# Gathers of the first graph layer: a wait for landed rows at every second block, and more blocks allowed ahead

## The chip, the cores and the metric

The kernel runs on one core of a Trainium2 chip. The metric is the device time of one execution in microseconds (us). Five engines work side by side: TensorE (PE), VectorE (DVE), ScalarE (ACT), GpSimd (POOL) and SyncE (SP), each with its own instruction stream, tied together by semaphores.

## The reference

Two graph layers over 12,500 nodes with 64 features and 400,000 edges, sorted by target node. Cut to what matters for the change, the first layer is:

```python
h0 = relu(layernorm(x))
src_feats = h0[src]                                   # one row per edge
h = concat([src_feats, edge_attr_32]) @ W1 + b1       # 400000 x 64
h = silu(layernorm(h) * g1 + be1)
messages = silu(h @ W2 + b2)
agg = segment_sum(messages, dst, 12500)
x = x + layernorm(silu(concat([agg, h0]) @ Wu + bu))
```

The second layer gathers and sums rows again and applies a two-matrix network. The change does not touch it.

## The kernel before, in words

The kernel first multiplies the node rows with the node part of W1 and stores the product as a table in HBM (`ptab`, "layer0_rows"). Layer 0 then needs, per edge, the table row of its source node plus the product of its 32 edge features.

The edges are cut into 391 blocks of 1024 (128 partitions by 8 columns, `BC` = 8). Block n uses slot s = n % 4 (`UN` = 4) of its buffers. The code is unrolled: `rounds` (L836) calls `step(e, j)` for eight blocks at a time, and each engine's `step` handles the block that is `lag` blocks behind (`lagged`, L824). The order of the work on each engine is thus written out by hand, and semaphores that count blocks tie the engines.

What each engine does for block n:

- SP (L885 to L892) loads the edge features, 128 KB, into slot s of `ea`, once the edge sums that read the slot have been made (`g_ep`).
- GpSimd (L896 to L906) waits until `g_z` (blocks whose edge sums are ready) has reached n - AHEAD + 1, with AHEAD = 2 (L872): the sums of block n - 2 have been made. Then `gather` (L737 to L742) issues eight indirect DMAs, each of which fetches 128 rows of 256 bytes into one column of slot s of `gat`. Each adds 16 to `g_gat[s]` when it has landed. The indices come from ACT, four blocks at a time (L803), two rounds ahead.
- PE multiplies the edge features (`edge_products`, L748, four matmuls); eight blocks later it transposes the normalised rows (L755, four), ten blocks later it makes the second product (L762 and L765, nine), thirteen blocks later it sums the messages into a window of target nodes (L772, eight). All of that is in one fixed order in `step` (L919 to L939).
- DVE adds the edge product in PSUM and the gathered rows (`z_ready`, L1000 to L1010; this is what raises `g_z`), which needs `g_ep` and `g_gat[s]`; it also takes the sums of squares of four blocks (L990), normalises (L1031), makes one-hot columns (L779) and adds the window sums (L812, L816).
- ACT squares four blocks at once (L953), applies the two silu functions (L967, L974) and converts indices (L803).

So a block's edge sum on DVE at L1008 needs two things: the gathered rows and PE's product of L748. GpSimd in turn needs an edge sum before it may go on.

```python
                        wait(pool, g_z, n - AHEAD + 1)
                        wait_alone(pool, "gpsimd")
                        gather(pool, ptab, j // UN, s, g_gat[s])
```

`wait_alone` raises a semaphore of its own, so that the wait stands on an instruction of its own.

Of the kernel before, what the change touches and what calls it, by code (L numbers as in the profile page):

```python
# [16 lines left out]
def build_gnn(nc, x, src, dst, src_rows, dst_rows, dst_heads, head_cols, edge_quads, W1, b1, g1, be1, W2, b2, Wu, bu, gn, bn, M1, c1, M2, c2, out):  # L17
# [8 lines left out]
    BLOCKS, BC = src.shape[1], src.shape[2]  # L26
# [36 lines left out]
    with ctx:  # L63
# [27 lines left out]
        def sem(name):  # L91
            return ctx.enter_context(nc.semaphore(name))
# [151 lines left out]
        def wait(eng, semaphore, value):  # L244

            if not isinstance(value, int) or value > 0:
                eng.wait_ge(semaphore, value)  # L247
# [10 lines left out]
        def wait_alone(eng, name):  # L258


            if name not in turns:
                turns[name] = sem(f"turns_of_{name}")
            eng.sem_inc(turns[name], 1)
# [473 lines left out]
        def gather(pool, table, half, j, done):  # L737

            for c in range(BC):
                pool.indirect_dma_start(  # L740
                    out=gat[:, j, c, :], out_offset=None, in_=table[:, :],
                    in_offset=bass.IndirectOffsetOnAxis(ap=idx[:, half, j, c:c + 1], axis=0)).then_inc(done, 16)  # L742
# [81 lines left out]
        def lagged(e, j, lag):  # L824

            return (j - lag) % UN, e * DB + j - lag

        def rows_before(e, j):

            return 2 * e + j // UN  # L830

        def there(n):

            return not isinstance(n, int) or 0 <= n < BLOCKS

        def rounds(step, lag):  # L836

            whole = BLOCKS // DB
            for e in range(whole):
                for j in range(DB):  # L840
                    step(e, j)
            for j in range(BLOCKS - whole * DB + lag):
                step(whole, j)

        def flagged(eng):
            return eng.value_load(flag[0:1, 0:1], min_val=0, max_val=1)
# [4 lines left out]
        g_gat = [sem(f"rows_gathered{j}") for j in range(UN)]  # L851
# [17 lines left out]

        NORMED, TURN, HID, SECOND, MSG, HOT, WSUM, WADD = 6, 8, 9, 10, 11, 11, 13, 14  # L870
        EARLY = 1
        AHEAD = 2  # L872

        def whole_round(e, j, back):

# [6 lines left out]
        with nc.Block() as block:  # L882
# [11 lines left out]
            @block.gpsimd  # L894
            def _(pool):
                def step(e, j):  # L896
                    s, n = lagged(e, j, 0)
                    if there(n):
                        if s == 0:
                            wait(pool, g_idx, rows_before(e, j) + 1)  # L900

                        wait(pool, g_z, n - AHEAD + 1)
                        wait_alone(pool, "gpsimd")
                        gather(pool, ptab, j // UN, s, g_gat[s])
                with pool.If(flagged(pool) == 0):
                    rounds(step, 0)  # L906

# [75 lines left out]
            def _(v):  # L983
                def squares_summed(e, j):

                    _, q = whole_round(e, j, 1)
                    if in_rounds(q):
                        wait(v, g_sq, q + 1)
                        wait(v, g_n, q * UN)
                        v.tensor_reduce(st[:, 0, :], sq[:, :, :, :].rearrange("p j c f -> p (j c) f"), X,  # L990
                                        ALU.add).then_inc(g_red, 1)

                def chain(e, j, k):

                    _, q = whole_round(e, j, 1)
                    if in_rounds(q):
                        wait(v, g_ra if k else g_red, q * RSTD + k if k else q + 1)
                        rstd_step(v, k, st[:, 0, :], st[:, 1, :], st[:, 2, :]).then_inc(g_ra, 1)
# [837 lines left out]
```

## Time and profile before

| what | value |
|---|---|
| median of 3 runs | 6933.1 us (6923.75 to 6956.05) |
| the profiled execution | 6930.31 us |
| span of its instructions | 6928.6 us |
| mean granted TensorE clock | 0.691 of full speed |
| GpSimd busy | 4280.7 us, 62% of the span |
| PE busy | 4087.1 us, 59% |
| DVE busy | 2515.7 us, 36% |
| ACT busy | 1807.5 us, 26% |
| GpSimd gathers of L740, both layers | 3992, 4050.5 us |
| HBM traffic over the span | 31 GB/s on average |

A page of the profile lists busy times by engine, the span in 40 slices, DMA queues, the chain that ended last and the costliest groups of instructions. Busy time on GpSimd here is the time in which it issues indirect DMAs. Other views list the instructions of one engine in order of time, each with the idle time ahead of it and what ended that idle time ("<-"); "issue" is idle time in which the engine waited for nothing that the profile shows, "remote" is a wait that ended with a semaphore whose writer the profile does not name. "Busy in a stretch" views give each engine's busy time and, in brackets, its number of instructions in a window of time.

### The profile page before, as it was taken

How to read it: one execution, taken by the hardware profiler on the slowest of the kernel's cores; microseconds unless marked ns; L12 is line 12 of the kernel's file. 1: busy time of each engine (PE TensorE's matmuls, PEld its weight loads, DVE VectorE, ACT ScalarE, POOL GpSimd, SP SyncE). 2: the span in 40 equal slices, each digit the busy share in tenths (PEclk: the TensorE clock that was granted, in tenths of full speed). 3: DMA queues.
4: the chain of work that ended last, by engine and by line, in shares of the span. 5: the costliest groups of instructions: out<-in, count | busy, mean ns of one | idle time of the engine just before them, and what ended most of it. 6: DMA issues, size and time to landing. Idle time of an engine off the chain costs nothing. (4 is left out here: it accounts for less than half of the span.)

```text
span 6928.6 us, 75131 instructions
## 1 busy us (share of the span) xinstructions
PE 4087.1 (59%) x24926; PEld 3298.2 (48%) x24926; DVE 2515.7 (36%) x5227; ACT 1807.5 (26%) x2517; POOL 4280.7 (62%) x4190
## 2 busy tenths in 40 slices
PE   5344544544554544555455455456658888788789
PEld 4233333433443433333334333335547777777776
DVE  5222222222222222222222222223656666566551
ACT  1011111111111111111111111111246555555551
POOL 3766666666666666666666666664456655556551
PEclk9556656666665666666566666666579999999995
DMA  2111111111111111111111111111110000000001
GB/s 84 42 34 34 34 34 34 35 33 34 34 35 33 35 34 34 35 34 35 33 34 34 33 35 35 33 34 23 40 23 18 18 17 16 17 17 17 17 17 34
DMA packets 257339, 216.92 MB, mean 31 GB/s; under 512 B 139070, under 2 KB 189563, under 8 KB 256617
## 3 DMA queue, kind: packets, MB, share of 16 engines
q0 software_dynamic: 133248, 136.74, 9.1%
q1 hardware_dynamic: 123881, 77.59, 3.9%
q8 instruction: 106, 1.74, 0.1%
q14 instruction: 104, 0.85, 0.0%
HBM read 199.53 MB, written 14.40 MB: 31 GB/s over the span
## 5 line engine op out<-in xcount | busy, mean ns | idle before, releaser
L740 POOL DMA_INDIRECT gat<-layer_rows,idx x3992 | 4050.5, 1015 | 2172.5 <-issue 1207.8
L765 PE MATMUL ps<-w2d,edge_buffers 128*128 128x128 f32 x3128 | 718.5, 348 | 868.9 <-issue 853.6
L1008 DVE TENSOR_TENSOR edge_buffers<-ps,gat 128x512 f32<-128x512 f32 x391 | 270.5, 692 | 2454.5 <-remote 1428.9
L1568 ACT ACTIVATE node_buffers<-ps 125x800 bf16<-125x800 f32 x1152 | 947.0, 838 | 703.8 <-PE ps L1619 553.5
L765 PEld LDWEIGHTS ps<-w2d,edge_buffers 128*128 128x128 f32 x3128 | 561.7, 241 | 1071.1 <-issue 1070.6
L772 PE MATMUL ps<-one_hots,edge_buffers 128*128 128x80 f32 x3128 | 604.4, 326 | 563.8 <-issue 543.2
L772 PEld LDWEIGHTS ps<-one_hots,edge_buffers 128*128 128x128 f32 x3128 | 593.4, 252 | 645.2 <-issue 615.5
L748 PE MATMUL ps<-w1e,edge_buffers 128*128 128x256 f32 x1564 | 616.0, 509 | 395.8 <-issue 263.1
L967 ACT ACTIVATE edge_buffers<-ps,gcol 128x512 f32<-128x512 f32 x391 | 302.6, 774 | 2088.1 <-remote 1730.9
L1619 PE MATMUL ps<-node_buffers 128*128 128x200 bf16 x4608 | 644.3, 265 | 333.3 <-ACT node_buffers L1568 188.3
L1598 PE MATMUL ps<-edge_buffers,node_buffers 125*128 125x192 bf16 x7200 | 811.5, 256 | 1.7 <-issue 1.2
L1598 PEld LDWEIGHTS ps<-edge_buffers,node_buffers 125*128 125x128 bf16 x7200 | 704.7, 142 | 16.5 <-issue 14.8
L1675 DVE TENSOR_TENSOR node_buffers<-iol,node_buffers 128x1024 bf16<-128x1024 bf16 x576 | 399.3, 693 | 633.4 <-PE ps L1619 454.1
L748 PEld LDWEIGHTS ps<-w1e,edge_buffers 128*128 128x128 f32 x1564 | 366.1, 255 | 521.9 <-issue 484.1
L1619 PEld LDWEIGHTS ps<-node_buffers 128*128 128x128 bf16 x4608 | 412.6, 102 | 420.0 <-issue 256.4
L755 PE MATMUL ps<-ident,node_buffers 128*128 128x128 f32 x1564 | 354.9, 329 | 402.5 <-issue 396.3
L1677 DVE TENSOR_TENSOR node_buffers<-ioh,node_buffers 128x1600 bf16<-128x1600 bf16 x576 | 567.8, 986 | 0.0
L974 ACT ACTIVATE edge_buffers<-ps 128x512 f32<-128x512 f32 x391 | 233.0, 596 | 976.7 <-remote 795.6
L755 PEld LDWEIGHTS ps<-ident,node_buffers 128*128 128x128 f32 x1564 | 241.1, 182 | 446.0 <-issue 443.3
L812 DVE TENSOR_TENSOR cT<-cT,ps 64x40 f32 x499 | 92.9, 186 | 901.8 <-remote 615.8
L953 ACT ACTIVATE node_buffers<-edge_buffers 128x2048 f32<-128x2048 f32 x98 | 187.2, 1910 | 837.1 <-DVE edge_buffers L1008 717.2
L1031 DVE TENSOR_TENSOR node_buffers<-edge_buffers,st 128x512 f32<-128x512 f32 x391 | 267.7, 685 | 3.3
(186 smaller groups left out, 2952.4 us busy)
## 6 DMA issues: line engine op xcount, KB each, us to landing
gat<-layer_rows,idx POOLq DMA_INDIRECT x3992
edge_buffers<-in_edge_quads SPq DMA_DIRECT2D x391, 128.0 KB
node_buffers<-in_x SPq DMA_DIRECT2D x5, 625.0 KB
layer_rows<-node_buffers SPq DMA_DIRECT2D x25, 125.0 KB
residual_rows<-node_buffers SPq DMA_DIRECT2D x5, 625.0 KB
layer_rows<-node_buffers SPq DMA_DIRECT2D x5, 625.0 KB
node_buffers<-residual_rows POOLq DMA_DIRECT2D x25, 125.0 KB, 4.4
out<-node_buffers SPq DMA_DIRECT2D x25, 125.0 KB
```

The source lines that it names most:

```text
L740: pool.indirect_dma_start(out=gat[:, j, c, :], out_offset=None, in_=table[:, :], in_offset=bass.IndirectOffsetOnAxis(ap=idx[:, half, j, c: ...
L748: mm = pe.matmul(o[:, k * 4 * F:(k + 1) * 4 * F], ea[:, j, k, :], w1e[:, :], start=True, stop=True)
L755: mm = pe.transpose(o[:, k * 128:(k + 1) * 128], zn[:, j, 2 * k:2 * k + 2, :].rearrange("p c f -> p (c f)"), ident[:, :])
L765: mm = pe.matmul(o[:, k * 128:(k + 1) * 128], hT[:, j, k * 128:(k + 1) * 128], w2d[:, :], start=False, stop=(k == PAIRS - 1), skip_group_c ...
L772: mm = pe.matmul(to[:, 0:2 * WIN], rows_of[:, 2 * k:2 * k + 2, :].rearrange("p c f -> p (c f)"), oh[:, j, 2 * k:2 * k + 2, :].rearrange("p ...
L967: a.activation(hT[:, s, :], tp[(j - HID) % 2][:, 0:PAIRS * 128], ACT.Silu, bias=gcol[:, 1:2], scale=gcol[:, 0:1]).then_inc(g_h, 1)
L1008: v.tensor_tensor(zb[:, j // UN % 2, s, :, :], zp[j % 2][:, 0:BC * F].rearrange("p (c f) -> p c f", c=BC), gat[:, s, :, :], ALU.add).then_ ...
L1568: a.activation(cnt[0:TP, s, ch * 8 * T:(ch + 1) * 8 * T].rearrange("p (b k) -> p b k", b=2), built[ch % 2][0:TP, :, :], ACT.Copy).then_inc ...
L1598: mm = pe.matmul(wide, cnt[0:TP, s, t:t + (GW - 1) * T + 1:T], hparts[:, t, :, :].rearrange("p k f -> p (k f)"), start=(t == 0), stop=(t = ...
L1619: mm = pe.matmul(built[ch % 2][:, i // 2, (i % 2) * 2 * T:(i % 2 + 1) * 2 * T], ohl[:, ch // 2 % 2, k // 2, :, k % 2], ohk[:, ch // 2 % 2, ...
L1675: v.tensor_tensor(ohl[:, g % 2, :, :, :], iol[:, :, :].unsqueeze(1).broadcast_to([128, GP // 2, 128, 2]), spread(keyl, d, g, 128), ALU.is_ ...
L1677: v.tensor_tensor(ohk[:, g % 2, :, :, :], ioh[:, :, :].unsqueeze(1).broadcast_to([128, GP // 2, 2 * T, 2]), spread(keyh, d, g, 2 * T), ALU ...
```

## The change

AHEAD goes from 2 to 4: the gathers of block n now wait for the edge sums of block n - 4 (whose slot of `gat` they overwrite) in place of those of block n - 2. And after the gathers of every block with an odd slot (n = 1, 3, ..., 389, 195 blocks) GpSimd waits until that block's eight gathers have landed, before it goes on to the next block.

```diff
         NORMED, TURN, HID, SECOND, MSG, HOT, WSUM, WADD = 6, 8, 9, 10, 11, 11, 13, 14
         EARLY = 1
-        AHEAD = 2
+        AHEAD = 4
...
                         wait(pool, g_z, n - AHEAD + 1)
                         wait_alone(pool, "gpsimd")
                         gather(pool, ptab, j // UN, s, g_gat[s])
+                        if s % 2 and n + 1 < BLOCKS:
+
+                            wait(pool, g_gat[s], rows_before(e, j) * (16 * BC) + 16 * BC)
                 with pool.If(flagged(pool) == 0):
                     rounds(step, 0)
```

`rows_before(e, j)` is the number of earlier blocks in the same slot, so the value waited for is that of the block just issued.

## Rows read from the trace of the kernel before

**Rows 1.** The page: busy time by engine, and the costliest gather and matmul groups.

```profile
PE 4087.1 (59%) x24926; PEld 3298.2 (48%) x24926; DVE 2515.7 (36%) x5227; ACT 1807.5 (26%) x2517; POOL 4280.7 (62%) x4190
...
L740 POOL DMA_INDIRECT gat<-layer_rows,idx x3992 | 4050.5, 1015 | 2172.5 <-issue 1207.8
L765 PE MATMUL ps<-w2d,edge_buffers 128*128 128x128 f32 x3128 | 718.5, 348 | 868.9 <-issue 853.6
```

**Rows 2.** Busy in a stretch, by stage: start, layer 0, its tail, the rest.

```profile
core 0: us, PE busy (x) PEld busy (x) DVE busy (x) ACT busy (x) POOL busy (x), PEclk, DMA share, GB/s
211.00:342.00 131.00, 35.39 (x90) 22.23 (x90) 19.85 (x42) 7.67 (x8) 98.66 (x104) 0.55 0.16 41
342.00:1000.00 658.00, 322.92 (x1377) 248.78 (x1378) 173.79 (x456) 101.61 (x141) 430.73 (x440) 0.60 0.14 34
1000.00:4772.00 3772.00, 1875.21 (x8057) 1417.02 (x8055) 999.30 (x2650) 579.28 (x804) 2524.16 (x2585) 0.62 0.14 34
4772.00:4800.00 28.00, 24.05 (x98) 19.84 (x98) 17.31 (x50) 9.89 (x13) 0.00 (x0) 0.50 0.06 3
4800.00:6929.00 2129.00, 1697.06 (x14550) 1483.65 (x14550) 1174.49 (x1833) 1069.63 (x1488) 1140.23 (x991) 0.84 0.10 21
```

**Rows 3.** The line of the gathers, L740, 205 to 4775 us: idle time ahead of them.

```profile
L740 POOL DMA_INDIRECT gat<-layer_rows,idx x3128: 941/947/1449, 211.5 to 4771.0; - x196
its engine sat idle before it (us, times) until:
  issue: 956.8, 3029
  DVE edge_buffers L1008: 550.1, 98
  ACT idx L803: 6.5, 1
```

**Rows 4.** POOL in order of time: the stops after runs of 24, 32 and 40 gathers.

```profile
2047.74 0.95 POOL L740 DMA_INDIRECT gat<-layer_rows,idx  x1 [0.30 <-issue]
2053.69 1.04 POOL L740 DMA_INDIRECT gat<-layer_rows,idx  x1 [5.00 <-DVE edge_buffers L1008]
...
2113.18 0.95 POOL L740 DMA_INDIRECT gat<-layer_rows,idx  x1 [7.41 <-DVE edge_buffers L1008]
...
2160.00 0.94 POOL L740 DMA_INDIRECT gat<-layer_rows,idx  x1 [5.98 <-DVE edge_buffers L1008]
...
2169.43 0.94 POOL L740 DMA_INDIRECT gat<-layer_rows,idx  x1 [0.30 <-issue]
```

**Rows 5.** Busy in a stretch, L740 alone: gathers in the runs before those stops.

```profile
core 0: us, POOL busy (x), PEclk, DMA share, GB/s
2113.00:2155.00 42.00, 31.39 (x32) 0.62 0.15 35
...
2018.00:2049.00 31.00, 23.25 (x24) 0.67 0.16 38
2053.00:2106.00 53.00, 38.73 (x40) 0.60 0.15 37
```

**Rows 6.** PE's pace after a stop that ended at 2113 us (columns as in rows 2).

```profile
2113.00:2123.00 10.00, 10.00 (x57) 8.48 (x56) 7.06 (x21) 2.07 (x4) 7.69 (x8) 0.80 0.16 39
2123.00:2133.00 10.00, 4.90 (x23) 3.33 (x23) 1.99 (x5) 2.69 (x3) 7.56 (x9) 0.71 0.15 37
2133.00:2144.00 11.00, 3.54 (x12) 2.60 (x10) 1.69 (x3) 0.60 (x1) 8.56 (x9) 0.50 0.16 39
2144.00:2154.00 10.00, 1.80 (x5) 0.93 (x5) 0.00 (x0) 0.00 (x0) 7.56 (x9) 0.50 0.12 26
```

**Rows 7.** PE and DVE in order of time: a product, and edge sums.

```profile
2177.09 1.44 PE L748 MATMUL ps<-w1e,edge_buffers 128*128 128x256 f32 x3 [0.42 <-issue]
...
2158.53 0.69 DVE L1008 TENSOR_TENSOR edge_buffers<-ps,gat 128x512 f32<-128x512 f32 x1 [1.86 <-remote]
...
2171.88 0.69 DVE L1008 TENSOR_TENSOR edge_buffers<-ps,gat 128x512 f32<-128x512 f32 x1 [3.57 <-DMA gat<-layer_rows,idx]
...
2205.31 0.69 DVE L1008 TENSOR_TENSOR edge_buffers<-ps,gat 128x512 f32<-128x512 f32 x1 [9.49 <-remote]
```

**Rows 8.** POOL and DVE in order of time: the stop at 342 us, after 104 gathers.

```profile
340.60 0.95 POOL L740 DMA_INDIRECT gat<-layer_rows,idx  x1 [0.31 <-issue]
358.76 1.04 POOL L740 DMA_INDIRECT gat<-layer_rows,idx  x1 [17.21 <-DVE edge_buffers L1008]
```

**Rows 9.** POOL and PE in order of time: a short stop at 3266 us.

```profile
3267.96 1.03 POOL L740 DMA_INDIRECT gat<-layer_rows,idx  x1 [1.96 <-issue]
...
3263.68 0.29 PE L772 MATMUL ps<-one_hots,edge_buffers 128*128 128x80 f32 x1 [0.90 <-issue]
3265.09 0.49 PE L772 MATMUL ps<-one_hots,edge_buffers 128*128 128x80 f32 x1 [1.12 <-issue]
3267.88 0.29 PE L772 MATMUL ps<-one_hots,edge_buffers 128*128 128x80 f32 x1 [2.29 <-issue]
3269.29 0.48 PE L772 MATMUL ps<-one_hots,edge_buffers 128*128 128x80 f32 x1 [1.12 <-issue]
3269.98 0.47 PE L755 MATMUL ps<-ident,node_buffers 128*128 128x128 f32 x1 [0.20 <-issue]
3270.68 0.37 PE L755 MATMUL ps<-ident,node_buffers 128*128 128x128 f32 x1 [0.22 <-issue]
```

## The prediction

> **What bounds the kernel now.** I read the page first, then the stages, then the gather line, then GpSimd, PE and DVE in order of time. The page shows no engine above 62% [rows 1], so a mean says little. The stages do: from 211 to 4772 us GpSimd issues the 3128 gathers of layer 0, and the rest of the kernel, which the change leaves alone, follows [rows 2]. Layer 0 is thus 4561 us, or 11.66 us for each of 391 blocks.
>
> GpSimd sets that pace. The gather line shows 3128 gathers and 956.8 + 550.1 + 6.5 = 1513.4 us of idle time ahead of them [rows 3]. Within a run the gap is 0.30 or 0.31 us; 3128 × 0.305 = 954 us is therefore the plain cost of going from one gather to the next. The other **559 us are stops**, nearly all ended by DVE's edge sum of L1008, 98 times. The rest, 4561 - 559 = 4002 us, is issue: 1.28 us per gather, 10.2 us per block. Extra per block now: 559 / 391 = 1.43 us, in stops of 5 to 7.4 us, about one every four blocks [rows 4].
>
> Why does the edge sum come late? Not for the rows: the last gather of a block ends at 2170.37 (2169.43 + 0.94) [rows 4] and its edge sum begins at 2171.88, released by the DMA [rows 7]: 1.51 us. It is late through PE. In the ten us after a stop PE starts 57 matmuls, then 23, then 12 in eleven us, then 5, while GpSimd issues at the same rate throughout [rows 6]. A block needs 25 (four of L748, four of L755, nine of L762 and L765, eight of L772), so 2.4 per us. PE keeps well ahead for 20 us of a run (80 matmuls, 3.2 blocks' worth) and then falls to a fifth of what is needed. Its idle time is "issue": it waits for nothing shown. What it reports is late as well: a product of L748 whose last matmul ends at 2178.5 releases an edge sum at 2205.31, marked "remote" [rows 7], 4.5 us after GpSimd has stopped. I read this as a debt: gathers issued without pause load something that PE's stream also needs, and only a pause of GpSimd pays it off.
>
> The debt has a size. The stop is 5.00 us after 24 gathers, 5.98 after 32, 7.41 after 40 [rows 4, 5], and 17.21 after the 104 gathers [rows 2] of the start, when PE had little to do [rows 8]. From 24 to 32 that is 0.12 us per gather; from 24 to 104 it is 12.2 / 80 = 0.15. A block of eight gathers so owes 0.98 to 1.22 us of GpSimd's silence, whenever it is paid. Of today's 1.43 us per block the remainder, 0.2 to 0.45, is what each stop costs besides: the edge sum itself (0.69) and GpSimd's restart, 0.78 us from the end of the sum (2158.53 + 0.69) to 2160.00 [rows 4, 7].
>
> **The change, part by part.**
> *AHEAD = 4.* No instruction is added or removed; the wait of block n asks for the sums of n - 4. Their slot is the one to be overwritten, so nothing else has to be free. The 98 stops on L1008 lose their reason as long as PE is less than two more blocks late, some 20 us. What is late next is the sum of n - 4. Behind GpSimd's wait only its own gathers are queued; SP's edge loads and ACT's indices don't wait for it. This part alone takes no debt away: it would make runs longer and each stop longer too.
> *The wait for landed rows*, 195 of them. No row shows GpSimd waiting for a DMA, so I bound it. From the end of a block's last issue to its release of DVE is 1.51 us [rows 4, 7]; GpSimd's restart after DVE adds 0.78 us, and the gap of 0.30 is there anyway. Upper value: 1.51 + 0.75 - 0.31 = 1.95 us. Lower value, if the restart lies inside the wait: 1.51 - 0.31 = 1.2, and the shortest stop shown, 1.96 us, would give 1.65 [rows 9]. I take 1.95, as every restart behind a semaphore in these rows has the 0.78. Sum: 195 × 1.95 = **380 us**. Queued behind it on GpSimd is the next pair's first gather; nobody else waits for it, since DVE has two landed blocks at that moment.
> *What it pays.* 380 us over 391 blocks is 0.97 us per block, against a debt of 0.98 to 1.22. The pauses come every 16 gathers, 20.5 us, the stretch in which PE still starts 80 matmuls against the 50 that two blocks need [rows 6]. So PE should stay in the good part of its curve. That a short pause helps is seen at 3266 us: with a stop of 1.96 us PE's matmuls go from 1.4 us apart to 0.7 us apart [rows 9], though it is not yet at full pace.
> *What is left over.* The unpaid part, 0.01 to 0.25 us per block, is 4 to 98 us, and comes as rarer stops on n - 4, each with some 1.5 us of its own (sum and restart). I take 50 us in all.
> *Clock, DVE, ACT, second layer:* PE's work in layer 0 is the same; its granted clock there is 0.60 to 0.62 [rows 2] between the two levels, and PE is not the bound, so nothing is charged. The tail from 4772 to 4800 stays.
>
> Sum: - 559 + 380 + 50 = - 129 us. Against the profiled execution, 6930.31 us, that is **about 6800**; it lies 3 us under the median of the runs, 6933.1.
>
> **A rule that speaks against it.** The row shows GpSimd held 1.51 us and a restart when it waits straight behind its issue. The Trainium skill ("DMA: Bandwidth & Descriptors", section "Rules for kernel authors") says to issue a DMA early, do other work, and wait on its semaphore late, so that the fixed cost overlaps; the change waits at once. The same page puts the fixed cost at about 2.0 us ("Anatomy of one DMA"); 195 times that is an estimate of 390 us added, with nothing given back. Whether that comes true is rival B, priced from rows.
>
> **The rivals.**
> *B: the pauses pay nothing, the stops stay (slower).* If a pause shorter than some 3 to 4 us does not release PE, PE still slows after 20 us of a run, whatever GpSimd does between. Place: the stops on L1008. They stay at one per four blocks with their length, since PE's rate per four blocks (some 100 matmuls per cycle of 2160.00 - 2113.18 = 46.8 us [rows 4]) hasn't changed, and AHEAD only shifts them. One of the two pauses per four blocks falls together with the stop, the other is added: 98 × 1.95 = 191 us, 7121 us. It decides from the point where PE's matmuls after a pause don't come closer together than before it. For it: at 3266 us PE didn't return to full pace after 1.96 us [rows 9]. Against: it doubled its pace, and that was after a long run, not after 16 gathers.
> *C: the debt is only moved (no change).* Each pause shortens the next stop by its own length, and the stops stay as frequent as PE's stock of 80 to 100 matmuls per run makes them. Then GpSimd's silence is the same 559 us: 6930. For it: the steady growth of the stop with the number of gathers, which knows no free payment.
> *D: the pauses do it all (faster still).* The debt never shows, there is no stop, and the wait costs 1.2 to 1.65 us: 559 - 234 to 559 - 380 less, 6605 to 6751. For it: in the first 131 us of layer 0 edge sums came on time for 13 blocks, while PE had few matmuls (90) [rows 2]. Against: the debt of at least 0.98 per block had to be paid in the end, 17.21 us [rows 8].
> That the change does nothing (the wait already satisfied when reached) is excluded: the wait stands behind the block's own issue, 1.5 us before it lands.
>
> **How the numbers follow.** Forecast 0.48; B 0.22; C 0.18; D 0.12. A measurement of this kernel can tell about 0.5%, 35 us, from no change. The forecast's own range is 6751 (nothing left over) to 6850 (98 us left over and its stops). The range asked for leaves out most of B above some 80 us and the lower part of D: 6690 to 7010. Faster by over 0.5%: forecast, D and an edge of C, 0.62. Within 0.5%: most of C and what joins from the forecast, 0.16. Slower: 0.22.
>
> **What would show it.** Right: GpSimd idle ahead of L740 in layer 0 about 1380 us in place of 1513; some 195 idle times of about 2.2 us ahead of a gather, released by the DMA or by "issue"; far fewer than 98 waits on L1008; PE's slices of ten us within layer 0 never down to 5 matmuls; the gathers of layer 0 end near 4640. Wrong: still 80 or more stops on L1008 of 5 us (B or C; C if they have become shorter by 2 us), or idle times of 3 us and more at the new wait, which would mean that landing reports are late in such runs too. Everything behind layer 0 must keep its 2129 us.

## The result, and the profile after

| | kernel before | changed kernel |
|---|---|---|
| median of the runs taken with the result | 6928.43 us (4 runs) | 6839.0 us (4 runs, 6821.14 to 6840.21) |
| ratio, 95% interval | | 0.9865 [0.9822, 0.9908] |
| the profiled execution | 6930.31 us | 6821.14 us |
| first to last gather of layer 0 | 4560.4 us | 4489.4 us |

The change makes the kernel 1.35% faster, about 90 us, in the direction and inside the range that were forecast (6800 in 6690 to 7010), with a gain about two thirds of the 129 us of the sum.

The changed kernel, busy by stage, answers to [rows 2] (L1008 has become L1011 here, the later lines are three further down too):

```profile
core 0: us, PE busy (x) PEld busy (x) DVE busy (x) ACT busy (x) POOL busy (x), PEclk, DMA share, GB/s
211.00:342.00 131.00, 36.03 (x96) 22.94 (x97) 19.62 (x42) 8.27 (x9) 91.82 (x96) 0.54 0.16 39
1000.00:4701.00 3701.00, 2160.11 (x7973) 1645.87 (x7973) 1001.54 (x2640) 571.86 (x795) 2536.79 (x2578) 0.56 0.14 35
4701.00:4749.00 48.00, 43.47 (x289) 36.78 (x290) 28.05 (x86) 19.55 (x27) 1.32 (x2) 0.86 0.04 4
```

The line of the gathers in layer 0 of the changed kernel, against [rows 3]:

```profile
L740 POOL DMA_INDIRECT gat<-layer_rows,idx x3128: 938/944/1443, 211.1 to 4699.6; - x196
its engine sat idle before it (us, times) until:
  issue: 1100.1, 2999
  DVE edge_buffers L1011: 191.8, 71
  DMA gat<-layer_rows,idx: 125.1, 57
  ACT idx L803: 5.6, 1
```

Idle time is 1422.6 us in place of 1513.4. With the plain 954 us taken off, GpSimd's silence has gone from 559 to **469 us**. Counted over the 3128 gathers, only 13 gaps of over 2.6 us are left, 61.7 us together (before: 97, 569.6 us), none of them between 1870 and 4113 us. Eight of the 13 stand at a new wait; the other 187 pauses have a median of 2.22 us from the end of a gather to the next. So most of the 71 waits that the view puts down to L1011 are pauses too, like the second one below.

GpSimd and DVE in order of time in the changed kernel: two pauses, a small gap after the first gather of a pair, and edge sums.

```profile
2145.08 1.38 POOL L740 DMA_INDIRECT gat<-layer_rows,idx  x1 [2.23 <-issue]
...
2167.71 1.38 POOL L740 DMA_INDIRECT gat<-layer_rows,idx  x1 [2.26 <-DVE edge_buffers L1011]
2170.51 0.94 POOL L740 DMA_INDIRECT gat<-layer_rows,idx  x1 [1.42 <-issue]
...
2144.36 0.69 DVE L1011 TENSOR_TENSOR edge_buffers<-ps,gat 128x512 f32<-128x512 f32 x1 [6.07 <-DMA gat<-layer_rows,idx]
2156.69 0.69 DVE L1011 TENSOR_TENSOR edge_buffers<-ps,gat 128x512 f32<-128x512 f32 x1 [10.31 <-DMA gat<-layer_rows,idx]
2166.99 0.69 DVE L1011 TENSOR_TENSOR edge_buffers<-ps,gat 128x512 f32<-128x512 f32 x1 [8.28 <-DMA gat<-layer_rows,idx]
```

The pair takes 22.63 us, and in these rows the edge sums wait for their gathered rows, as they should, and no longer for TensorE. Its pace in ten-us slices, against [rows 6]:

```profile
2100.00:2110.00 10.00, 5.40 (x25) 4.45 (x25) 1.01 (x4) 4.86 (x7) 7.73 (x8) 0.67 0.15 37
2110.00:2120.00 10.00, 7.07 (x25) 5.67 (x25) 2.05 (x5) 0.60 (x1) 7.55 (x8) 0.50 0.16 36
2120.00:2130.00 10.00, 5.30 (x17) 3.72 (x17) 4.95 (x9) 1.37 (x2) 6.11 (x6) 0.50 0.10 23
2130.00:2140.00 10.00, 6.99 (x26) 5.49 (x25) 3.63 (x14) 0.00 (x0) 7.76 (x8) 0.50 0.17 39
```

Here PE has 17 to 26 in each, at half clock for most of the time, and that is enough. Counted from 340 us on over the whole of layer 0, the slow slices have become rare but are not gone: of 435 slices, 80 have 12 matmuls or fewer (before: 210) and 10 have 5 or fewer (before: 86).

Where the 109 us between the two profiled executions come from: 71 from first to last gather of layer 0; about 7 behind its last gather (TensorE's backlog is smaller: the last matmul of L772 starts 50 us after the last gather ended before, 44 after); 33 from the first to the last gather of layer 1 (1647.9 us before, 1615.0 after). The change leaves layer 1's code alone, and another profile of the changed kernel has 1661.8 there, so the last term is scatter and no gain. (Behind the gathers of layer 1 the changed kernel takes 2 us more, which closes the sum.)

### The profile page after: what moved, and what is told of

It is laid out like the page before. It is cut to its first block and busy times, and to the rows that moved or that the text cites. A ratio compares the mean times of both kernels' runs of the same rounds, so it can differ in the third digit from the quotient of the medians.

```text
span 6819.3 us, 75228 instructions
## 1 busy us (share of the span) xinstructions
PE 4384.2 (64%) x24926; PEld 3521.7 (52%) x24926; DVE 2520.6 (37%) x5227; ACT 1807.0 (26%) x2517; POOL 4292.5 (63%) x4190
## 5 line engine op out<-in xcount | busy, mean ns | idle before, releaser
L740 POOL DMA_INDIRECT gat<-layer_rows,idx x3992 | 4061.0, 1017 | 2057.2 <-issue 1349.3
L748 PE MATMUL ps<-w1e,edge_buffers 128*128 128x256 f32 x1564 | 736.4, 608 | 988.0 <-DVE edge_buffers L1011 770.5
L1011 DVE TENSOR_TENSOR edge_buffers<-ps,gat 128x512 f32<-128x512 f32 x391 | 270.5, 692 | 2831.4 <-DMA gat<-layer_rows,idx 1590.4
L748 PEld LDWEIGHTS ps<-w1e,edge_buffers 128*128 128x128 f32 x1564 | 424.7, 298 | 1154.1 <-issue 1095.4
L765 PE MATMUL ps<-w2d,edge_buffers 128*128 128x128 f32 x3128 | 759.3, 390 | 328.3 <-issue 321.6
L772 PE MATMUL ps<-one_hots,edge_buffers 128*128 128x80 f32 x3128 | 693.1, 380 | 390.3 <-issue 241.7
L772 PEld LDWEIGHTS ps<-one_hots,edge_buffers 128*128 128x128 f32 x3128 | 676.4, 298 | 516.4 <-issue 478.1
L765 PEld LDWEIGHTS ps<-w2d,edge_buffers 128*128 128x128 f32 x3128 | 618.4, 279 | 512.6 <-issue 512.1
L755 PE MATMUL ps<-ident,node_buffers 128*128 128x128 f32 x1564 | 387.5, 376 | 182.5 <-issue 178.4
L755 PEld LDWEIGHTS ps<-ident,node_buffers 128*128 128x128 f32 x1564 | 292.7, 217 | 215.7 <-issue 215.1
```

Source lines behind the costliest of these rows:

```text
L740: pool.indirect_dma_start(out=gat[:, j, c, :], out_offset=None, in_=table[:, :], in_offset=bass.IndirectOffsetOnAxis(ap=idx[:, half, j, c: ...
L748: mm = pe.matmul(o[:, k * 4 * F:(k + 1) * 4 * F], ea[:, j, k, :], w1e[:, :], start=True, stop=True)
L755: mm = pe.transpose(o[:, k * 128:(k + 1) * 128], zn[:, j, 2 * k:2 * k + 2, :].rearrange("p c f -> p (c f)"), ident[:, :])
L765: mm = pe.matmul(o[:, k * 128:(k + 1) * 128], hT[:, j, k * 128:(k + 1) * 128], w2d[:, :], start=False, stop=(k == PAIRS - 1), skip_group_c ...
L772: mm = pe.matmul(to[:, 0:2 * WIN], rows_of[:, 2 * k:2 * k + 2, :].rearrange("p c f -> p (c f)"), oh[:, j, 2 * k:2 * k + 2, :].rearrange("p ...
L1011: v.tensor_tensor(zb[:, j // UN % 2, s, :, :], zp[j % 2][:, 0:BC * F].rearrange("p (c f) -> p c f", c=BC), gat[:, s, :, :], ALU.add).then_ ...
```

## The experiments

The experiments were run on five chips, and each ran beside the kernel before on its own chip; only those pairs are compared.

**1. AHEAD = 4 alone** (against the kernel before).

```diff
-        AHEAD = 2
+        AHEAD = 4
```

> AHEAD = 4, no wait for landed rows. Debt theory (every gather issued without pause adds 0.12 to 0.15 us to a debt that only silence of GpSimd pays): the silence per block stays at 0.98 to 1.22 us plus the fixed part of each stop, so the gain is small: 0 to 60 us under the kernel before, 6870 to 6930; the stops are longer (7 to 9 us) and fewer. Rival, more blocks allowed ahead is what gained: the whole 90 us, about 6840. Rival C (PE has a fixed stock per stop): no change, stops as frequent as before.

Measured: 5996.86 us beside a kernel before of 5998.14, ratio 1.0022 [0.9944, 1.0100]. On this chip both kernels take some 930 us less than the kernel before took in the first measurement. The gathers of layer 0 in this run:

```profile
L740 POOL DMA_INDIRECT gat<-layer_rows,idx x3128: 940/944/1397, 211.9 to 4191.8; - x196
its engine sat idle before it (us, times) until:
  issue: 953.0, 3127
  ACT idx L803: 5.8, 1
```

There is no stop at all: 3127 plain gaps, 953 us, just the plain cost of the prediction. And the same four stretches of TensorE as in [rows 6]:

```profile
2113.00:2123.00 10.00, 7.99 (x28) 5.81 (x27) 3.54 (x14) 0.00 (x0) 7.87 (x8) 0.58 0.19 39
2123.00:2133.00 10.00, 5.52 (x25) 4.29 (x25) 1.99 (x5) 5.64 (x8) 7.56 (x9) 0.77 0.19 37
2133.00:2144.00 11.00, 5.65 (x25) 4.74 (x25) 2.17 (x6) 1.37 (x2) 8.26 (x10) 0.66 0.18 38
2144.00:2154.00 10.00, 6.53 (x22) 4.92 (x23) 4.96 (x10) 0.00 (x0) 7.56 (x9) 0.50 0.19 40
```

TensorE starts 22 to 28 matmuls in each of them, with gathers issued at the same rate. Over the whole of layer 0 no slice of ten us has 5 or fewer, and 14 of 384 have 12 or fewer. Neither the clock nor the DMA traffic makes the difference: the granted clock in these slices is 0.50 to 0.77, as on the other chip (0.50 to 0.80), and the traffic 37 to 40 GB/s (there 26 to 39). So the slowing beside uninterrupted gathers doesn't come from the kernel alone but from the chip it meets. Each chip was measured at one time only, so a lasting property of the chip and a passing state of it aren't told apart. I call this one the free chip, the others the bound chips. Which kind a run met can be read from its kernel before: 6000 or 6920 to 6950 us.

**2. The wait alone, the wait at every block, and the wait at every third block,** all on the free chip. The edits are against the changed kernel:

```diff
-        AHEAD = 4
+        AHEAD = 2
```

> The wait at every second block with AHEAD = 2. Debt theory: the pauses pay, PE is hardly late, so the edge sums of n - 2 are there in most of the layer: within 40 us of the changed kernel, 6800 to 6880. Rival, both halves are needed: the sums of n - 2 are late again and again, each costing a stop on top of the pauses: 6930 or more.

```diff
-                        if s % 2 and n + 1 < BLOCKS:
+                        if n + 1 < BLOCKS:
```

> AHEAD = 4, the wait at every block, 390 pauses of 1.92 us beyond the plain gap = 749 us against 464 us of stops in the changed kernel. Debt theory: no stops left at all, and the layer costs 749 - 464 = 285 us more than the changed kernel: about 7120. Rival (more silence also speeds something else, PE being the limit): less than 100 us more.

```diff
-                        if s % 2 and n + 1 < BLOCKS:
+                        if n % 3 == 2 and n + 1 < BLOCKS:
```

> AHEAD = 4, the wait at every third block: 130 pauses of 1.92 = 250 us, 0.64 us per block, less than the debt of 0.98. Debt theory: the steady stretch without stops is gone, stops return until the silence per block is 1.0 to 1.3 again, time 6830 to 6900. Rival (what counts is that a pause comes at all, not how much is paid): no stops, 214 us less than the stops of the changed kernel, about 6630.

| run, free chip | us | ratio to the kernel before | gathers of layer 0, first to last | more than without pauses, per pause |
|---|---|---|---|---|
| AHEAD = 4 alone | 5996.86 | 1.0022 [0.9944, 1.0100] | 3980.9 | |
| 130 pauses | 6275.48 | 1.0521 [1.0380, 1.0661] | 4257.5 | 2.13 us |
| 195 pauses, AHEAD = 2 | 6493.62 | 1.0886 [1.0740, 1.1031] | 4477.3 | 2.55 us |
| 390 pauses | 6861.18 | 1.1500 [1.1347, 1.1654] | 4845.6 | 2.22 us |

None of the expectations for a bound chip could be judged here, but the price could: where nothing has to be paid, a pause is a plain loss of 2.1 to 2.6 us, somewhat over the 1.95 of the prediction. The pause itself is 1.99 us beyond the plain gap; in the run with 195 of them the other 0.56 us per pause are longer gathers behind it (the first one takes 1.38 us in place of 0.94) and 32 small gaps of 1.41 us ahead of the gather after that. With 195 pauses layer 0 takes 4477 us on the free chip and 4489 in the changed kernel on a bound one: with them, the two kinds of chip are alike in layer 0.

**3. The changed kernel again,** unchanged, to see whether the gain was the chip's.

> The changed kernel as it is, beside the kernel before on one chip, since the first four runs stood beside a kernel before of 5998 us in which the gathers never stopped. If the slow pace of TensorE is a state of the chip on which it runs and this chip does not show it: the pauses cost 195 x 1.95 us and pay for nothing, ratio 1.06 to 1.09, some 6380 to 6500 against 6000. If this chip shows it: ratio 0.98 to 0.99 as in the first measurement. Rival: what differed was the kernel before alone, and the change gives 6839 anywhere.

Measured, on a bound chip: 6845.73 against 6941.77 us, ratio 0.9855 [0.9808, 0.9901]. The first result is repeated. The changed kernel itself was not run on the free chip; that the rival ("6839 anywhere") falls is argued from the wait alone, which takes 6494 us there.

**4. AHEAD = 4 alone and the wait alone, on a bound chip.**

> AHEAD = 4 without the wait, once more, for a chip on which the kernel before takes some 6930 us and TensorE slows beside the gathers. Debt theory: silence per block stays 1.0 to 1.3 us, stops longer (7 to 9 us) and fewer, ratio 0.991 to 1.000. Rival, AHEAD alone is the gain: ratio 0.986. Rival, a fixed stock of TensorE per stop: 1.00 with as many stops as before. Where the kernel before takes 6000 us again: ratio 1.00 and no stops.

> The wait at every second block with AHEAD = 2, once more, for a chip of the slow kind. Debt theory: the pauses pay and the edge sums of n - 2 are there in most of the layer, ratio 0.982 to 0.992. Rival, the room of two more blocks is needed as well: the late sums cost stops on top of the pauses, ratio 1.00 or above. On a chip of the fast kind: 1.08 to 1.09.

Measured on one chip, kernel before 6923.12: AHEAD alone 6917.11 (a difference of 6 us, where the runs of each kernel spread over more than 100 us), the wait alone 6855.08, ratio 0.9905 [0.9883, 0.9927]. The gathers of layer 0 with AHEAD alone:

```profile
L740 POOL DMA_INDIRECT gat<-layer_rows,idx x3128: 940/944/1464, 211.8 to 4765.6; - x196
its engine sat idle before it (us, times) until:
  issue: 1163.6, 3058
  DVE edge_buffers L1008: 376.2, 69
  ACT idx L803: 5.7, 1
```

and with the wait alone:

```profile
L740 POOL DMA_INDIRECT gat<-layer_rows,idx x3128: 938/944/1452, 215.9 to 4706.8; - x196
its engine sat idle before it (us, times) until:
  issue: 1065.6, 2989
  DVE edge_buffers L1011: 203.8, 81
  DMA gat<-layer_rows,idx: 129.1, 57
  ACT idx L803: 5.7, 1
```

AHEAD alone leaves 98 gaps of over 2.6 us with a median of 6.33 us and a silence of 1545.5 - 954 = 592 us, no less than before. The runs between stops stay at four blocks (55 of 97) with more fives and threes. The wait alone leaves 9 such gaps and a silence of 450 us. From first to last gather layer 0 takes 4492 us with the wait alone, 4489 and 4496 in two profiles of the changed kernel. **The wait is the change; AHEAD adds nothing that these runs can tell.** The rival "room is needed as well" falls too.

**5. Silence in small pieces, first attempt.** No wait for rows, AHEAD = 4, a one-element clear on GpSimd ahead of every second gather:

```diff
             for c in range(BC):
+                if spaced is not None and c % 2:
+                    pool.memset(spare[c // 2 * 32:c // 2 * 32 + 1, spaced:spaced + 1], 0.0)
```

> AHEAD = 4, no wait; instead GpSimd clears one element ahead of every second gather, four per block, so that the silence is spread in small pieces of 0.3 to 0.6 us. It adds 4 x 0.3 to 4 x 0.6 = 1.2 to 2.4 us per block. On a chip of the slow kind, debt theory (any silence pays, in whatever pieces): no stops of several us are left, the layer takes 3128 x 1.28 us plus the pieces, ratio 0.987 to 1.05. Rival (only an unbroken pause in which the last gather has landed releases TensorE): the stops stay, 559 us besides the pieces, ratio 1.07 to 1.13. On a chip of the fast kind it shows the price of the pieces alone.

Measured: 6940.71 against 6923.12 us, ratio 1.0030 [1.0012, 1.0048], and 96 gaps of over 2.6 us (median 6.38). It does not test the question: a clear takes 0.095 us and in most places hides in the plain gap of 0.30; the gaps with a clear come to 50 us more than as many plain ones, nearly all of it in 31 gaps of over 1 us. With no pieces paid, the stops stay.

**6. Pieces that cost time.** A copy of 200 bf16 elements per partition ahead of every fourth gather:

```diff
             for c in range(BC):
+                if spaced is not None and c % 4 == 3:
+                    wait(pool, s_spare, 2 * spaced + c // 4 + 1)
+                    pool.tensor_copy(spare[:, 200:400], spare[:, 0:200]).then_inc(s_spare, 1)
```

> AHEAD = 4, no wait for landed rows; GpSimd copies 200 bf16 elements per partition ahead of every fourth gather, two per block, since the one-element clears of the run with spaced gathers hid in the plain gap. Each copy should part two gathers by some 0.5 to 0.8 us more than the plain gap: 1.0 to 1.6 us per block in pieces in which the last gather has not landed. Debt theory on a chip of the slow kind: the pieces pay, fewer than 20 stops of over 2.6 us, layer 0 takes 4002 us plus 391 x 1.0 to 1.6. Rival (only an unbroken pause until the rows have landed releases TensorE): some 95 stops stay beside the pieces, 7300 or more.

GpSimd in order of time, a piece and a stop (the gathers' line is L746 here):

```profile
2111.48 0.94 POOL L746 DMA_INDIRECT gat<-layer_rows,idx  x1 [0.30 <-issue]
2112.43 0.35 POOL L745 COPY spare<-spare 128x200 bf16<-128x200 bf16 x1
2112.95 0.97 POOL L746 DMA_INDIRECT gat<-layer_rows,idx  x1 [0.17 <-issue]
2118.63 1.04 POOL L746 DMA_INDIRECT gat<-layer_rows,idx  x1 [4.70 <-DVE edge_buffers L1016]
```

A piece adds 0.22 us to the plain gap, a third of what I had expected: 782 of them, 188 us in all with the few longer ones. Measured: 6933.29 against 6953.33 us, ratio 0.9991 [0.9962, 1.0021]. The profiled execution is the shortest of the eleven (6839.91 us), but what it lacks lies behind the last gather of layer 1 (128 us, against 200 to 226 in the other profiles), so its layer 0 can be compared: 4580 us from first to last gather, against 4560 before. There are 72 gaps of over 2.6 us, 391.6 us, against 97 and 569.6. So about 180 us of stops went for 188 us of pieces: exchanged about one for one. Neither expectation is met: the stops neither vanish nor stay.

**7. Every third block, on a bound chip.**

> The wait at every third block, AHEAD = 4, once more, for a chip of the slow kind. 130 pauses of 1.95 us are 0.65 us per block, under the debt of 0.98 to 1.22. Debt theory: the long stretches without stops of the changed kernel are gone, 40 to 90 stops of over 2.6 us come back, the silence per block lies at 1.1 to 1.4 us, 6860 to 6920. Rival (each pause renews TensorE's stock, however rarely it comes): fewer than 20 such stops, 6720 to 6760.

Measured: 6939.37 against 6953.33 us, ratio 0.9986 [0.9960, 1.0011].

```profile
L740 POOL DMA_INDIRECT gat<-layer_rows,idx x3128: 942/947/1455, 214.5 to 4784.9; - x196
its engine sat idle before it (us, times) until:
  issue: 1101.9, 3021
  DVE edge_buffers L1011: 381.4, 77
  DMA gat<-layer_rows,idx: 66.9, 29
  ACT idx L803: 7.0, 1
```

81 gaps of over 2.6 us are back, as the debt theory has it, and the rival (each pause renews everything) falls. But the silence, 1557.2 - 954 = 603 us or 1.54 per block, is above the 1.1 to 1.4 I had set, and the time is above the 6860 to 6920: paying two thirds of what the changed kernel pays bought nothing.

**8. Less work for TensorE,** AHEAD = 2, no wait; the products of three of the four pairs of L765 are left out, so the messages are incomplete.

```diff
-            for k in range(PAIRS):
-                mm = pe.matmul(o[:, k * 128:(k + 1) * 128], hT[:, j, k * 128:(k + 1) * 128], w2d[:, :],
-                               start=False, stop=(k == PAIRS - 1), skip_group_check=True)
-            return mm
+            return pe.matmul(o[:, 0:128], hT[:, j, 0:128], w2d[:, :], start=False, stop=True, skip_group_check=True)
```

> The kernel before (AHEAD = 2, no wait) with seven of the eight matmuls of the second product (L765) left out: 18 matmuls per block on TensorE in place of 25; the messages come out incomplete. On a chip of the slow kind: if TensorE gets a stock of some 100 matmuls per stop of GpSimd and a trickle besides, the runs between stops grow from 4 blocks to 5 or 6 (40 to 48 gathers), each stop is 1 to 2 us longer, and the silence per block falls from 1.43 to 1.1 to 1.3 us: 6820 to 6890. Rival (what ends a run is the number of gathers, whatever TensorE does): runs of 4 blocks as before, about 6930. Second rival (TensorE's own work was the bound): the time falls by far more than 100 us.

The product of one pair is two matmuls in the trace, so six of the eight are gone and not seven, and a block has 19 matmuls in place of 25, one more than the expectation says. Measured: 6861.44 us in one run, kernel before 6937.54. GpSimd in order of time, two stops that follow each other:

```profile
2051.55 0.94 POOL L740 DMA_INDIRECT gat<-layer_rows,idx  x1 [7.22 <-DVE edge_buffers L1005]
...
2109.41 1.00 POOL L740 DMA_INDIRECT gat<-layer_rows,idx  x1 [7.03 <-issue]
```

The run between them, from the start of the first gather to the end of the last, is 50.8 us long. Of 79 runs 63 are now of five or six blocks (38 and 25), where the kernel before has 75 of 96 of four; the median stop is 6.97 us in place of 5.87. So what ends a run is how much TensorE has executed since the last stop, some 100 matmuls (4 blocks of 25, or 5.4 of 19), and not the number of gathers. The place at which its pace breaks says the same: in the runs of four blocks of the kernel before it starts, on average, only 4 matmuls or fewer per 5 us from 20 us behind the stop on, after 80 matmuls; here that comes at 30 us in the runs of five blocks, after 79, and at 40 us in the runs of six, after 91. A slowing that grew with the gathers or with time alone would have come at the same place. The silence, 1487.5 - 954 = 534 us or 1.36 per block, is a little above the 1.1 to 1.3 I expected. Between this profile and that of the kernel before (6930.31 us) 47 of the 69 us lie between the first and the last gather of layer 0; layer 1, which this edit leaves alone, has 22.

**9. The same wait in layer 1,** on top of the change, as the experiments pointed there: on a bound chip the 864 gathers of layer 1 have 60 gaps of over 2.6 us (371.2 us), on the free chip none.

```diff
                     gather(pool, htab, 0, j, g_gat[j])
+                    wait(pool, g_gat[j], r * (16 * BC) + L0_ROWS + 16 * BC)
```

> The changed kernel, and in layer 1 too GpSimd waits after each block's gathers until they have landed (108 pauses of some 1.95 us = 210 us). In the kernel before, layer 1's gathers stop 78 times for 411 us on a chip of the slow kind and never on one of the fast kind. Slow kind, debt theory: the pauses take the place of the stops, layer 1 shrinks from 1660 us to about 1530, in all 6690 to 6760. Rival (the stops in layer 1 come from TensorE's full queue of matmuls and stay): 6840 to 7050. Fast kind: 200 us more than the changed kernel there, 6700.

Measured: 6812.78 against 6937.54 us, ratio 0.9817 [0.9778, 0.9855]. The gathers of layer 1 in this run:

```profile
L740 POOL DMA_INDIRECT gat<-layer_rows,idx x864: 938/996/3217, 5002.5 to 6599.7; - x173
its engine sat idle before it (us, times) until:
  issue: 270.5, 767
  ACT idx L792: 250.3, 55
  DMA gat<-layer_rows,idx: 97.2, 41
  PE ps L772: 2.4, 1
```

It is the fastest version measured on bound chips, but it is only 26 and 33 us below the two medians of the changed kernel, each on another chip; that is less than expected (6690 to 6760), and the intervals of the ratios overlap. Layer 1 takes 1598 us from first to last gather where the changed kernel takes 1615 and 1662. 60 gaps of over 2.6 us are still there, only shorter (259.6 us). It was not run on the free chip, where layer 1's gathers run back to back (1312 us) and pauses can be expected to cost there as in layer 0.

## Why the prediction was right, and where it was off

**What bounds the kernel.** Right on the bound chips: layer 0 is GpSimd's plain issue plus stops, and the stops come from TensorE's slow pace beside gathers. The free chip shows the plain cost by itself: 953 us of gaps and no stop, where the prediction had worked out 954. What I did not say, and no row of one profile could say, is that the slow pace depends on the chip.

**The wait, 380 us.** Taken at 1.95 us each; measured 2.22 us from gather to gather, less the plain 0.305: 1.92, or 374 us. The upper value was the right choice: in the rows above, the edge sum starts 1.51 us after the last gather ended (2142.85 to 2144.36) and GpSimd goes on 0.72 us later. (The sum put 0.75 for this restart, where its own row gives 0.78; that is 6 us.) The Trainium skill gives about 2.0 us as the fixed cost of such a transfer ("DMA: Bandwidth & Descriptors", "Anatomy of one DMA"). That is near the pause of 2.22 us seen here, though not near its first part alone, the 1.51 us. The Trainium skill's advice on the same page to wait late ("Rules for kernel authors") is what the free chip bears out, with 5 to 15% lost; on the bound chips the runs disagree with it (ratio 0.9905 for the wait alone).

**What is left over, 50 us.** This is the term that was mis-sized. Measured silence 469 us, less 374: 95 us. The 13 stops make some 58 us, but eight of them stand in the place of a pause that the 374 already hold, so they add 42. Another 42 us are 32 small gaps, mostly of 1.41 or 1.86 us, one in twelve blocks, ahead of the second gather of a pair. They belong to the wait and not to TensorE's lateness: on the free chip the runs with 195 and 390 pauses have 32 of them as well, and AHEAD = 4 alone has none. The prediction had no term for them. The other 11 us are the wait for the first indices and three more gaps. One small thing besides: the mean gather took 0.982 us in place of 0.976, 19 us over 3128, which I had not charged. Together 45 + 19 - 6 = 58 us: the difference between the 129 of the sum and the 71 that layer 0 gained.

**AHEAD = 4.** "Takes no debt away" was right. That it was needed so that the stops "lose their reason" was wrong: with AHEAD = 2 and the wait, 9 gaps of over 2.6 us were left. Once TensorE keeps pace, two blocks are enough.

**The debt.** I had it that silence pays in whatever portion, 0.98 to 1.22 us per block, and that a shortfall comes back as stops of that size. With full payment (195 pauses) the silence did come down, to 1.20 and 1.15 us per block, within those bounds. Partial payments show the other side: 1.54 with 130 pauses, and an even exchange with the copies. In other words, somewhere between 0.65 and 0.96 us per block there is a point below which the pauses only move the silence, which was rival C, and above which the stops go. That it is the dose that counts is not shown: with it the spacing changed too, a pause after every 24 gathers in place of 16. C's price (no change) was right for these variants, and its "stock" of 80 to 100 matmuls per run is what the run with fewer products shows, though pauses add to it: with the copies the runs of five blocks hold 118. The forecast held because the changed kernel lies above that point; nothing in the profile of before had said so, and that part was luck.

**The signs.** Of those named for "right", the pauses of 2.2 us and the rarer stops came. The idle time fell to 1423 us and not to 1380, and the last gather starts at 4700 us and not near 4640, both for the term above and the longer gathers. "Never down to 5 matmuls" failed in 10 slices.

**Rivals B and D.** B would have shown stops of the old length and number; 13 are left. D has no stop at all; that came for about half of layer 0, the 2243 us without one, but not for the rest.

**Left open.** What in the chip is shared between GpSimd's gathers and TensorE's stream, why one chip of the five of the experiments doesn't have it, and where between 0.65 and 0.96 us the point lies. A shorter pause at every second block was not tried, so it isn't shown either whether the rows must have landed or whether silence alone is enough. One candidate is made unlikely by the traces: queue 8 ("instruction") brings 80 loads of 16 KB during layer 0 before and on the free chip alike, in a median of 0.98 and 1.09 us, and 97 stops stand against these 80 loads, so the stops don't go one by one with loads of code.

## What to carry to other kernels

When an engine's instructions come ever further apart while it waits for nothing shown, look at what another engine issues without a break: a short forced pause there can be worth more than the time it costs. Here that took 195 pauses; 130 of them, or small pieces, merely moved the idle time. Measure such a change on more than one chip: this one gains 1.4% on those with the effect, and the same 195 pauses, without the larger AHEAD, lose 9% on the one without it. Change one knob at a time: half of this edit did nothing that could be measured.

## What was not expected of the hardware

The kernel before takes 5998 us on one chip and 6923 to 6953 us on the others. Read from the profile of AHEAD = 4 alone, which takes the same time there (5997 us), the difference is idle time ahead of gathers and nothing else that is large: first to last gather 3981 against 4560 us in layer 0 and 1312 against 1648 in layer 1, with the single gather of layer 0 no faster (median 0.944 and 0.947 us). A one-element clear on GpSimd between two gathers is nearly free (0.095 us, in most places inside a gap of 0.30), and a copy of 0.35 us adds only 0.22.

The first gather behind a pause takes longer: 1.38 us on average in the run with 195 pauses on the free chip, against 0.94 in the same places without the pauses.
